# Attention and experts on one core: values placed directly in front of sums, and the output projection as an fp32 matmul

## The reference

```python
xn = layernorm(x)                                # x: 32 x 256 x 128
q  = xn @ Wq.T                                   # 8 heads of 32
kv = xn @ Wkv_down.T                             # rank 64
k, v = kv @ Wk_up.T, kv @ Wv_up.T
attn = softmax(einsum('bqhd,bkhd->bhqk', q, k) * 32 ** -0.5)
att  = einsum('bhqk,bkhd->bqhd', attn, v).reshape(b, t, 256) @ Wo.T
idx  = floor(xn @ wr + br) mod 8                 # one of 8 experts per token
ffn  = relu(xn @ W1[idx] + b1[idx]) @ W2[idx] + b2[idx]
out  = x + att + ffn
```

## Time and profile before

| what | value |
|---|---|
| median of 3 runs | 561.96 us (561.79 to 564.86) |
| the profiled execution | 561.93 us, its span 560.1 us |
| mean granted TensorE clock | 0.969 of full speed |
| PE busy | 462.7 us (83%) |
| DVE busy | 471.7 us (84%) |
| ACT busy | 382.0 us (68%) |
| POOL busy | 392.3 us (70%) |

### The profile page before, as it was taken

One profiled execution on the slowest core, in us unless ns is written; L12 is line 12 of the kernel. 1 busy time (PEld: TensorE's weight loads), 2 busy tenths in 40 slices (PEclk: granted clock), 3 DMA queues, 4 the chain that ended last, 5 costly groups with the idle time before them and its releaser, 6 DMA issues.

```text
span 560.1 us, 15849 instructions
## 1 busy us (share of the span) xinstructions
PE 462.7 (83%) x5016; PEld 299.0 (53%) x5016; DVE 471.7 (84%) x1000; ACT 382.0 (68%) x957; POOL 392.3 (70%) x362
## 2 busy tenths in 40 slices
PE   0433444999999999998699999998989999999984
PEld 0222211545455455455499999996545545645532
DVE  4897749799999999989688888887698988988985
ACT  0767931576777777777577777775677867877784
POOL 4166740689889888944377777775977977978970
PEclk9999757899999999999999999999999999999998
DMA  7995363455456456444778888881544764755531
GB/s 187 291 380 200 143 156 76 91 131 122 109 120 133 108 116 134 106 86 103 232 215 272 266 260 265 272 254 50 133 100 104 146 127 112 146 120 117 106 82 49
DMA packets 84956, 87.08 MB, mean 155 GB/s; under 512 B 10433, under 2 KB 66337, under 8 KB 84897
## 3 DMA queue, kind: packets, MB, share of 16 engines
q1 hardware_dynamic: 80800, 77.92, 53.1%
q0 software_dynamic: 4096, 8.40, 6.6%
HBM read 38.94 MB, written 22.04 MB: 109 GB/s over the span
## 4 chain that ended last, share of the span: by engine, by line
PE 38%; DVE 18%; issue 17%; POOL 14%; DMA 4%; SPq 4%; ACT 3%; DVEq 1%; POOLq 1%; ACTq 0%
POOL split L444 12%; PE psum L1061 8%; PE psum L1091 8%; DVE negm L858 6%; PE psum L1075 6%; PE psum L1106 4%; PE psum L1012 3%; PE psum L1124 3%; PE psum L1013 3%; PE psum L1014 3%; DVE oTl L872 2%; DMA stk<-mT 2%; DVE split L757 2%; DVE acc L877 2%; SPq L286 1%
## 5 line engine op out<-in xcount | busy, mean ns | idle before, releaser
L598 ACT ACTIVATE prob<-psum 128x512 f32<-128x512 f32 x256 | 151.1, 593 | 94.4 <-PE psum L1075 93.3
L858 DVE TENSOR_REDUCE negm<-psum 128x2 f16<-128x512 f32 x256 | 172.8, 683 | 36.6 <-PE psum L1061 35.3
L490 POOL TENSOR_TENSOR padd<-prob 128x512 f32<-128x512 f32 x120 | 139.2, 1160 | 44.9 <-ACT prob L598 42.8
L1061 PE MATMUL psum<-stk 96*128 96x256 f16 x512 | 100.7, 279 | 12.4 <-DVE negm L858 11.3
L444 POOL TENSOR_TENSOR split<-xTl,split 128x512 f16<-128x512 f32 x72 | 83.3, 1157 | 33.1 <-DVE split L948 33.1
L667 ACT ACTIVATE xTl<-psum,xn_all 128x128 f32<-128x128 f32 x288 | 82.0, 368 | 28.2 <-POOL split L444 23.4
L1075 PE MATMUL psum<-stk 97*128 97x256 f16 x512 | 98.0, 273 | 3.3 <-DMA stk<-mT 2.9
L460 POOL DMA_INDIRECT xsort<-xn_all,pos x64 | 63.0, 984 | 31.2 <-DVE pos L840 19.1
L1061 PEld LDWEIGHTS psum<-stk 96*128 96x128 f16 x512 | 38.2, 99 | 72.0 <-DVE negm L858 33.4
L468 POOL DMA_INDIRECT xn_all<-ysort,pos x64 | 64.1, 1001 | 12.1 <-issue 8.9
L1091 PE MATMUL psum<-prob,vt 128*32 128x256 f32 x1024 | 68.5, 385 | 0.7 <-ACT prob L598 0.7
(11 more groups left out here) (143 smaller groups left out, 984.7 us busy)
## 6 DMA issues: line engine op xcount, KB each, us to landing
stk<-split SPq DMA_DIRECT2D x192, 128.0 KB
xn_all<-wsplit SPq DMA_DIRECT2D x72, 258.0 KB, 4.3
xsort<-prob SPq DMA_DIRECT2D x9, 512.0 KB, 6.4
xTh<-xsort SPq DMA_DIRECT2D x18, 256.0 KB, 3.9
ysort<-xTh SPq DMA_DIRECT2D x18, 256.0 KB, 4.1
stk<-W SPq DMA_DIRECT2D x16, 256.0 KB, 5.5
wsplit<-stk SPq DMA_DIRECT2D x16, 256.0 KB, 3.8
out<-acc SPq DMA_DIRECT2D x16, 256.0 KB
```

Source lines behind the costliest of these rows:

```text
L490: nc.gpsimd.tensor_tensor(padd[:, bb, hs], prob[:, bb, hs, 0, :], prob[:, bb, hs, 1, :], ALU.add).then_inc(pool_add, 1)
L598: nc.scalar.activation(prob[:, bb, h, :, :].rearrange("p a c -> p (a c)"), bank[2 + n % 2], ACT.Exp, scale=SCALE).then_inc(act_exp, 1)
L858: V.tensor_reduce(negm[:, k % 2, col:col + 2], bank[n % 2].rearrange("p (a c) -> p a c", a=2), AX.X, ALU.max, negate=True).then_inc(dve_ma ...
L1061: ins = mm(bank[n % 2][:, qc * T:(qc + 1) * T], stk[0:96, s, 1, h, t0 + qc * P:t0 + (qc + 1) * P], stk[0:96, s, 0, h, t0:t0 + T], start=Tr ...
```

## The change

The placement on PE changes: `values` and `sums` of one sequence now stand together, in step 7 for bb = 0 and in step 2 of the next unit (after `proj_q`) for bb = 1. The output projection takes the normalised values as fp32: `normalise` writes them straight into `oT`, `o_high` and `o_low` are gone, and `out_proj` is 8 fp32 matmuls with `oT` as the stationary and fp32 `wo_s` as the moving operand. `wo_s` is loaded by DMA; its cast and low part are gone, and `residual` needs no factor. The wait for the reuse of the block's buffer moves from ACT's `o_high` to DVE's `normalise`. Tables of the routing that lived in `oTh` and `oTl` live in `oT`.

```diff
-        oTh = sb("oTh", [P, 2, NG, SB], F16)
-        oTl = sb("oTl", [P, 2, NG, SB], F16)
+        oT = sb("oT", [P, 2, NG, SB], F32)
-        on = sb("on", [P, 2, T], F32)
-        wo_s = sb("wo_s", [P, 2, NG, D], F16)
+        wo_s = sb("wo_s", [P, NG, D], F32)
...
-                             (wo_f, woT), (b1c[:], b1T),
+                             (wo_s[:].rearrange("p g d -> p (g d)"), woT), (b1c[:], b1T),
...
-                        cast(wo_s[:, 0, :, :].rearrange("p g d -> p (g d)"), wo_f, WS)
...
-            def o_high(b, k, bb, s):
-
-                act.wait_ge(dve_on, b + 1)
-                if k % 2 == 0 and (not isinstance(s, int) or s >= 2):
-                    act.wait_ge(pe_wo, s - 1)
-                nc.scalar.activation(oTh[:, (k // 2) % 2, k % 2, bb * T:(bb + 1) * T], on[:, bb, :],
-                                     ACT.Copy).then_inc(act_oh, 1)
...
-                    if not f:
-                        o_high(u * 2 - 2, k + 3, 0, sb_prev)
...
-                    if not f:
-                        o_high(u * 2 - 1, k + 3, 1, sb_prev)
...
-            low(wo_s[:, 1, :, :].rearrange("p g d -> p (g d)"), wo_f,
-                wo_s[:, 0, :, :].rearrange("p g d -> p (g d)"), WS)
...
-            def normalise(b, par):
+            def normalise(b, par, k, s):
                 dve.wait_ge(act_rinv, b + 1)
-                if not isinstance(b, int) or b >= 2:
-                    dve.wait_ge(act_oh, b - 1)
-                    dve.wait_ge(dve_ol, b - 1)
-                V.tensor_tensor(on[:, par, :], bank[4 + par][:, 0:T], rinv[:, par, :], ALU.mult
-                                ).then_inc(dve_on, 1)
-
-            def o_low(b, k, bb):
-                dve.wait_ge(act_oh, b + 1)
-                dst = (slice(None), (k // 2) % 2, k % 2, slice(bb * T, (bb + 1) * T))
-                V.tensor_tensor(oTl[dst], on[:, bb, :], oTh[dst], ALU.subtract).then_inc(dve_ol, 1)
+                if par == 0 and k % 2 == 0 and (not isinstance(s, int) or s >= 2):
+                    dve.wait_ge(pe_wo, s - 1)
+                V.tensor_tensor(oT[:, (k // 2) % 2, k % 2, par * T:(par + 1) * T], bank[4 + par][:, 0:T],
+                                rinv[:, par, :], ALU.mult).then_inc(dve_on, 1)
...
-                V.scalar_tensor_tensor(a4, bank[7].rearrange("p (c d) -> p c d", c=4), 1.0 / WS, a4,
-                                       ALU.mult, ALU.add).then_inc(dve_acc, 1)
+                V.tensor_tensor(a4, bank[7].rearrange("p (c d) -> p c d", c=4), a4,
+                                ALU.add).then_inc(dve_acc, 1)
...
                 pe.wait_ge(dve_kl, kdone)
-                pe.wait_ge(dve_ol, 4 * s + 4)
+                pe.wait_ge(dve_on, 4 * s + 4)
                 for tc in range(4):
                     t = slice(tc * P, (tc + 1) * P)
-                    i = 0
                     for g in range(NG):
-                        for o, w in ((oTh, 0), (oTl, 0), (oTh, 1)):
-                            ins = mm(bank[7][:, t], o[:, sbp, g, t], wo_s[:, w, g, :], start=(i == 0), stop=(i == 5))
-                            i += 1
+                        ins = mm(bank[7][:, t], oT[:, sbp, g, t], wo_s[:, g, :], start=(g == 0), stop=(g == NG - 1))
...
-                        if n == 1 and not f:
-                            values(u * 2 - 1, k + 3, 1, it * 2 + (k + 1) // 2 * 2)
...
                         if n == 2 and not f:
+                            values(u * 2 - 1, k + 3, 1, it * 2 + (k + 1) // 2 * 2)
                             sums(u - 1, 1, last and k == 3)
...
-                        if n == 5:
-                            values(u * 2, k, 0, sbu * 2 + 1, u + 2 if nxt else u + 1)
...
                         if n == 7:
+                            values(u * 2, k, 0, sbu * 2 + 1, u + 2 if nxt else u + 1)
                             sums(u, 0, last and k >= 2)
```

More of the change, by code:

```diff
@@ L107, in attention_moe_block @@
         wq_f, wkup_f, wvup_f = prob_f[:, 1024:1280], prob_f[0:R, 1280:1536], prob_f[0:R, 1536:1792]
-        wkvd_f, wo_f = prob_f[0:R, 1792:1920], prob_f[:, 1920:2176]
+        wkvd_f = prob_f[0:R, 1792:1920]
         wr_f, br_f = prob_f[:, 2176:2304], prob_f[:, 2304:2305]
@@ L112, in attention_moe_block @@
         prod = padd_f[:, 0:1024].rearrange("p (a c d) -> p a c d", a=2, c=4)
-        oTh_f = oTh[:, :, :, :].rearrange("p a b c -> p (a b c)").bitcast(F32)
-        oTl_f = oTl[:, :, :, :].rearrange("p a b c -> p (a b c)").bitcast(F32)
+        oT_f = oT[:, :, :, :].rearrange("p a b c -> p (a b c)")
         keys, kf, kgt, ef = (padd_f[:, 1024 + 64 * i:1088 + 64 * i] for i in range(4))
         ki = padd_f[:, 1280:1344].bitcast(I32)
-        oh = oTh_f[:, 0:512].rearrange("p (e c) -> p e c", e=E)
-        cum = oTl_f[:, 0:512].rearrange("p (e c) -> p e c", e=E)
-        place = oTl_f[:, 512:1024].rearrange("p (e c) -> p e c", e=E)
+        oh = oT_f[:, 0:512].rearrange("p (e c) -> p e c", e=E)
+        cum = oT_f[:, 1024:1536].rearrange("p (e c) -> p e c", e=E)
+        place = oT_f[:, 1536:2048].rearrange("p (e c) -> p e c", e=E)
         rsm = padd_f[:, 1344:1472]
@@ L204, in attention_moe_block @@
         dve_on = sem("dve_on")
-        act_oh = sem("act_oh")
-        dve_ol = sem("dve_ol")
         pe_wo = sem("pe_wo")
@@ L268, in _ @@
                 if e == 3:
-                    sp.wait_ge(act_cast, 3)
+                    sp.wait_ge(act_cast, 2)
                     sp.dma_start(wsplit[:, :, F:W1E // 2].rearrange("e p c -> p e c"),
@@ L632, in body @@
                     nxt = not (last and k == 3)
-                    sb_prev = it * 2 + (k + 1) // 2 - 1
                     exp(u, 0, f)
@@ L680, in _ @@
                 recip(NU - 2 + bb, bb)
-                o_high(NU - 2 + bb, 3, bb, NSB // 2 - 1)
             for t in range(NT):
@@ L689, in _ @@
                 recip(2 * NU - 2 + bb, bb)
-                o_high(2 * NU - 2 + bb, 3, bb, NSB - 1)
         @block.vector
@@ L773, in _ @@
             variance(1)
-            dve.wait_ge(act_cast, 5)
+            dve.wait_ge(act_cast, 4)
             def low(dst, src, high, scale):
@@ L780, in _ @@
             low(wq_s[:, 1, :], wq_f, wq_s[:, 0, :], WS)
-            low(wo_s[:, 1, :, :].rearrange("p g d -> p (g d)"), wo_f,
-                wo_s[:, 0, :, :].rearrange("p g d -> p (g d)"), WS)
             low(b2s[32:32 + E, :], b2_f[32:32 + E, :], b2s[32:32 + E, :], WS)
-            dve.wait_ge(act_cast, 7)
+            dve.wait_ge(act_cast, 6)
             low(wk_s[:, 1, :], bank[6][:, 0:256], wk_s[:, 0, :], WS)
@@ L915, in body @@
                         if n == 2 and not f:
-                            normalise(u * 2 - 2, 0)
+                            normalise(u * 2 - 2, 0, k + 3, it * 2 + (k + 1) // 2 - 1)
                         if n == 3 and qk:
                             q_low(u + 3, k + 3)
-                        if n == 4 and not f:
-                            o_low(u * 2 - 2, k + 3, 0)
                         if n == 5 and not f:
-                            normalise(u * 2 - 1, 1)
+                            normalise(u * 2 - 1, 1, k + 3, it * 2 + (k + 1) // 2 - 1)
                         if n == 6 and half == 1 and not f and not (last and k == 3):
                             expert_sum(u - NU // 2 - 1, (k + 1) % 2)
-                        if n == 7 and not f:
-                            o_low(u * 2 - 1, k + 3, 1)
                         if n == 6 and k % 2 == 1 and not (first and half == 0 and k == 1):
@@ L958, in finish_unit @@
                 for bb in range(2):
-                    normalise(2 * u + bb, bb)
-                    o_low(2 * u + bb, 3, bb)
+                    normalise(2 * u + bb, bb, 3, u // 2)
             for n in range(8):
@@ L1035, in _ @@
                 if s == 11:
-                    pe.wait_ge(dve_ws, 5)
+                    pe.wait_ge(dve_ws, 4)
                     proj_q(0, 0, 0)
```

## The result

The kernel after takes 555.94 us (median of 4 runs, 555.80 to 556.69) against 561.88 us (4 runs, 561.40 to 564.86): a ratio of 0.989, interval 0.9868 to 0.9913. Timed again beside the last group of experiments it was 555.91 against 562.22 us, 0.9911 (0.9890 to 0.9932). So the change gives about 1%, with both intervals clear of 1. The profiled execution took 555.84 us, its span 554.0 us.

What follows compares the result with a forecast made beforehand. POOL was taken to bound units 1 to 12; in the second half PE was nearest its limit but waited on DVE. -0.3 - 1.9 + 0 - 3.6 - 0.6 = -6.4 us, from 561.93 to 555.5 us, range 549.5 to 562.5.

Steps and rivals of the forecast that it cites:

- Sum and stages: Whole kernel: start -0.3, units 0 to 12 -1.9, units 12 to 15 0, second half -3.6, end -0.6; -6.4 us.
- The projection: out_proj on PE: 8 fp32 matmuls as 16 records take 1.8 us instead of 1.34, 0.46 more every second unit.
- The lower bound: out_proj on PE: 1.78 us if all weight loads are hidden; the other bound was 2.7 us.
- the third rival: out_proj on PE: fp32 loads don't overlap matmuls, so 4.0 us a projection and about 587 us in all; chance 0.08.
- Entry and exit of the strips: values and sums on PE: putting a pair together saves 0.10 + 0.11 = 0.21 us, 0.42 us a unit.
- The walk through a unit: Second half, engine orders laid side by side with trace times: a pair takes 20.23 instead of 20.74 us, -3.6 over seven.
- two of the signs: Second half: no wait of proj_k for residual was expected; short units longer than 9.8 us would prove the forecast wrong.
- What leaves DVE and ACT: Removed o_low (0.62 us on DVE, two a unit) and o_high (0.41 us on ACT); called no pure gain.
- First half: Units 1 to 12: POOL stays full; -0.5 us from its additions and 1.4 us won once, together -1.9.
- The fourth rival: Units 1 to 12: POOL only in step with DVE through stretched o_low; units of 10.1 us, 551.4 in all; chance 0.10.
- First rival: Second half: packed steps cost no more than now, a pair 19.5 us, seven pairs -8.7, 550.4 in all; chance 0.15.
- the wait of step 2: Second half on PE: step 2 waits 0.28 us for step 0's maximum, a wait values used to cover.

Runs made afterwards that it cites:

- residual_first: Kernel after with residual ahead of expert_sum on DVE in step 6 of odd units; 560.08 us against 570.62 for the kernel before, 0.9827.
- the dummy: Kernel after with an unused operation of o_low's size given back to DVE in steps 4 and 7; 562.78 us, 1.0017 of the kernel before.
- that of `o_high`: Kernel after with an o_high-sized copy given back to ACT before the exponentials of steps 4 and 7; 558.59 us, 0.9945 of the kernel before.
- before_pool_less: Kernel before with POOL's small addition of units 0 to 15 moved into a wider DVE addition; 571.59 us, 1.0008 of the kernel before.
- proj_k_later: Kernel after with proj_k behind step 0's scores instead of in front; 558.34 us, 0.9800 of the kernel before.

## Why the prediction was right

- **Sum and stages.** -6.4 us was forecast and -6.1 us found in the profiled execution, and no stage is off by more than 0.35 us. Part of this is luck: a steady pair of units gave 0.39 us and not 0.51, the start and the experts scatter by as much as their differences, and the next points show more.
- **The projection.** 1.78 us against 1.8 taken. The lower bound, all loads hidden, is the true one, and the third rival (4.0 us) is out. The estimate worked out in the prediction from the Trainium skill, "TensorE: Matmul & The Clock Gate", sections "LDWEIGHTS" and "The mechanism", 3.5 us, does not hold here: 16 full-array fp32 loads, recorded with 199 ns each, and their 16 matmul records take 1.78 us together, so they overlap though they use the same rows of the array. The same section "The mechanism" also says that a load into the background weight buffer is pulled ahead of running matmuls. The prediction left this out; the measured number agrees with it.
- **Entry and exit of the strips.** 0.89 us for `values` with `sums` behind it, in the loop as at the end, as forecast.
- **The walk through a unit.** For the kernel after it gave 9.49 and 10.74 us; measured were 9.46 and 10.99. The missing 0.25 us of the long unit is `residual`'s wait, which I had at zero: I counted `expert_sum` with 0.60 us, its pace in the earlier trace rows, and in the new order it meets one of POOL's additions and takes 1.01 us in these units. `residual_first` gives the 0.30 us. So two of the signs that I had named failed: `proj_k` still waits, and two units inside the stretch pass the 9.8 us that I had called wrong for short ones (9.88 and 9.92; the first one, 10.82, was 11.03 before). Seven steady pairs give 2.7 us; the forecast of the whole stretch was met because the transition from unit 29 to 30 gave 0.89 us by itself.
- **What leaves DVE and ACT.** Here the reasoning was thin. I called it no pure gain and gave it no price of its own, while the walk silently had it gone. The prices are now known: 0.64 us a short unit for `o_low` (10.10 against 9.46, up to 0.1 in the long one) and 0.18 for `o_high`. In my text the gain of the second half looked like that of the placement. The placement alone gives none, since the packed steps bring `o_low` onto the path: that run and the dummy have the same short unit, 10.10 us.
- **First half.** POOL stays full, and now PE waits for it, both as said. Most of my 1.9 us was that PE gets ahead once by 1.4 us, and the trace has 1.26 us won once, in the first three units and not where POOL's load ends. The rest, 0.5 us from shorter operations of POOL, is 0.3 us in the other nine units. But placement alone kept 127.26 us there (32.21 in the first three units) and the projection alone gave 125.77 (29.44). With the dummy of `o_low` the three units take 33.33 us, with that of `o_high` 29.18. So the 1.6 us belong to the missing `o_low`, not to the order on PE, as far as one early unit can show it. The fourth rival (units at 10.1 us) did not come true for the kernel after. `before_pool_less` shows that POOL was not the only bound before; that the stretched `o_low` was the other one is not shown.
- **First rival.** Packed steps without cost did not happen: the wait of step 2 that the walk has, 0.28 us, is what `proj_k_later` takes away in the long unit beyond `residual_first`, 10.69 to 10.40 us.

## What to carry to other kernels

Where engines with in-order queues hand buffers of depth two to each other, a step costs what the slowest latency behind it makes of it, not its share of busy time (here 0.64 us a unit on an engine that is 77% busy): write the orders beside each other, put the trace's times in, and check the walk on the kernel before first. Walk each part of a change alone as well, since two edits can be worth something only together, here an order that needs the relief and a relief whose price is covered by the order. Where the trace shows operations stretched beside another engine's work, ask in the walk what each of them will stand beside in the new order: the time that it had in the old one can be too short.

## What was not expected of the hardware

The recorded duration of a weight load says little on what it costs: 199 ns a load at a pitch of 111 ns for fp32, 97 at 56 for fp16, both hidden. And `expert_sum`, DVE work with two SBUF inputs, went from 0.8 to 1.4 us on average without a change to it or to POOL's program. POOL's additions stretch it, to 1.82 us beside a whole one, and its gathers do not: 0.68 us beside a gather alone in the kernel before. POOL's large additions keep 1.26 to 1.30 us in the second half meanwhile. `o_low`, also with two SBUF inputs, goes the same way, from 0.42 us alone to 2.17 in the kernel before. This is read from overlaps in the timelines; no run was made for it alone.
